# GpSimd adds all thirteen probability tiles of a group, and the row sums share a ring of five PSUM banks

## The chip, the cores and the metric

One core of a Trainium2 chip runs the whole kernel as one launch. The metric is device time in microseconds (us), the median of three runs. TensorE is called PE, VectorE DVE, ScalarE ACT, GpSimd POOL and the sync engine SP, as the profile has them.

## What is computed

The reference is a gated block on x (8 batches of 512 rows, width 512) with a context of 1601 rows per batch:

```python
q = qdq(layernorm(x)) @ qdq(wq).T + bq
k, v = split(ctx @ wkv.T + bkv)
attn = softmax(q k / sqrt(32))            # 16 heads of 32
x = x + tanh(g_xattn) * (qdq(attn @ v) @ qdq(wp).T + bp)
x = x + tanh(g_ffn) * (moe(layernorm(x)) + shared(layernorm(x)))
```

The softmax needs, for each head and each of 512 queries, the sum of the exponentials over 1601 context rows. How this sum is made is what the change touches.

## The kernel before, in words

The attention works by batch (8), by group of four heads (4), and by step: a step is one tile of 128 context rows, so a group has KT = 13 steps and the last tile has 65 rows. "Group 4.1" is group 1 of batch 4; there are 32 groups. The order of all engines is written out by hand and every engine walks it in its own program, tied to the others by semaphores.

In a step PE makes four score tiles (line 786, `scores_of`, two PSUM banks `s_ps`), ACT takes the exponential of each (line 965, `exp_of`) into one of three slots of `probs`, and PE multiplies them with the values (line 800, `heads_of`, one step late) into `o_ps`. Beside that each step carries tiles of other work (`lead_tiles`, `fill_tiles`) for the group that comes next: its k pieces and q (lines 698, 687), 64 tiles of scores whose row maxima DVE takes (lines 708 and 1184, steps 3 to 11), the context's transposes, the values, the output projection. All these tiles share a ring of NBANKS = 4 PSUM banks `r_ps`: tile n of the order uses bank n mod 4, and PE waits in `open_tile` until the tile four before it has been read.

The row sums are made in two ways. For ten of the thirteen steps POOL adds the four `probs` tiles to `prob_acc` (`add_probs`: a copy at step 0, line 1436, else an add, line 1439). For steps 4, 8 and 12 PE multiplies the tiles with ones into the bank `sum_ps` (line 812, `sums_of`, four matmuls that stand as x8 in the profile). After a group, PE adds `prob_acc` in the same way (line 820, `accumulated_sums`), at the end of step 0 of the next group, and ACT copies the bank to `sum_sb` (line 975, `copy_sums`). Only then may POOL begin the copy of the next group, since it overwrites `prob_acc`. ACT may reuse a slot of `probs` when PE has read the tiles of three steps before, and, for the ten steps, when POOL has added them.

In the step where POOL has nothing to add, step 4 of group 0, it adds a bias to the x rows (line 1446, `add_bias`). After the last group SP waits for the last sums (line 570) before it reads rows back into `prob_acc` and loads the shared weights; the feed-forward part and 32 experts follow, on the same ring.

The lines that set this:

```python
SBANKS, NBANKS, HALVES = 2, 4, 3
POOL_STEPS = [kt for kt in range(KT) if kt not in (4, 8, KT - 1)]
FIRST_SUMS = 4
```

Of the kernel before, what the change touches and what calls it, by code (L numbers as in the profile page):

```python
# [18 lines left out]
ALU = mybir.AluOpType  # L19
# [20 lines left out]
EPS = 1e-5  # L40
ROUND = 12582912.0
CT_SLOTS = 3
SBANKS, NBANKS, HALVES = 2, 4, 3
POOL_STEPS = [kt for kt in range(KT) if kt not in (4, 8, KT - 1)]
FIRST_SUMS = 4
MAX_STEPS = range(3, KT - 1)
V_AHEAD = 6
V_AT = {6: 1, 7: 2, 8: 4, 9: 5, 10: 7, 11: 8, 12: 10}
# [11 lines left out]
def rows(t):  # L60

    return min(P, M - t * P)


def group(b, g):

    return b * GROUPS + g


def step_of(b, g, kt):  # L70

    return group(b, g) * KT + kt
# [19 lines left out]
def head_tiles(b, g):  # L92
    return [("oT", b, g), ("sumT", b, g)]
# [73 lines left out]
class Ring:  # L167


    def __init__(self):  # L170
        order = [("setup", name, c) for name in ("wqT", "wpT", "wkT", "wvT") for c in range(DC)]
        order += [("setup", "gateT"), ("setup", "swp")]
        order += first_tiles()
        for at in steps():
            order += lead_tiles(*at) + fill_tiles(*at)
        order += head_tiles(B - 1, GROUPS - 1) + [("hT", 0, c) for c in range(DC)] + [("logits", 0)]
        for f in range(B):
            order += ffn_tiles(f)
        order += [("hgT", 0)]
        for e in range(E):  # L180
            order += [("eg", e), ("eu", e)] + ([("hgT", e + 1)] if e + 1 < E else []) + [("ey", e)]
        assert len(set(order)) == len(order)
        self.n = {key: i for i, key in enumerate(order)}
# [37 lines left out]
def build(nc, x, ctx_in, g_xattn, g_ffn, wq, bq, wkv, bkv, wp, bp, gate_w, gate_bias, w1, w2, w3,  # L221
# [16 lines left out]
    with ctx:  # L238
# [3 lines left out]
        def sem(name):  # L242
            return ctx.enter_context(nc.semaphore(name))
# [118 lines left out]
        s_ps = [ctx.enter_context(nc.psum_tensor(f"s_ps{j}", [P, 512], FP32)) for j in range(SBANKS)]  # L362
        r_ps = [ctx.enter_context(nc.psum_tensor(f"r_ps{i}", [P, 512], FP32)) for i in range(NBANKS)]
        o_ps = ctx.enter_context(nc.psum_tensor("o_ps", [P, 512], FP32))
        sum_ps = ctx.enter_context(nc.psum_tensor("sum_ps", [P, 512], FP32))


        consts_ready = sem("consts_ready")
# [33 lines left out]
        probs_ready = sem("probs_ready")  # L402
        probs_used = sem("probs_used")
        probs_added = sem("probs_added")
        acc_summed = sem("acc_summed")
        heads_copied = sem("heads_copied")
        sums_copied = sem("sums_copied")
        h_ready = sem("h_ready")
        h_out = sem("h_out")
        x1_out = sem("x1_out")  # L410
# [36 lines left out]
        def _(sp):  # L447
# [119 lines left out]

            sp.wait_ge(x_quantised, B)
            sp.dma_start(xin[:, :, :], x_v[B - 1]).then_inc(x_again, DMA)
            sp.wait_ge(acc_summed, B * GROUPS)  # L570
            ffn_in(0)
            for wt, src in ((sg, shared_gate), (su, shared_up), (sd, shared_down)):
                sp.dma_start(wt[:, :, :], src.rearrange("(c p) n -> p c n", p=P)).then_inc(shared_in, DMA)
# [31 lines left out]
        def _(pe):  # L605
# [43 lines left out]
            def tile(key):  # L649
# [67 lines left out]
                    for t in range(TT):  # L717
                        last = nc.tensor.transpose(ps[:, t * P:(t + 1) * P], oT_sb[:, t * P:(t + 1) * P], ident[:, :])
                elif kind == "sumT":
                    pe.wait_ge(sums_copied, group(b, key[2]) + 1)  # L720
                    ps = open_tile(*key)
                    for t in range(TT):
                        last = nc.tensor.matmul(ps[:, t * GH:(t + 1) * GH], sum_sb[:, t * P:(t + 1) * P],
# [65 lines left out]
            def heads_of(s):  # L789

                kt, b, g = s % KT, s // KT // GROUPS, s // KT % GROUPS
                w, slot = rows(kt), s % HALVES
                if kt == 0 and s:
                    pe.wait_ge(heads_copied, s // KT)
                if g == 0:
                    wait_read(pe, "v", b, kt)
                pe.wait_ge(probs_ready, s * GH + GH)
                for j in range(GH):
                    h = g * GH + j
                    last = nc.tensor.matmul(o_ps[j * DH:(j + 1) * DH, :], v_sb[0:w, kt, h * DH:(h + 1) * DH],  # L800
                                            probs[0:w, slot, j, :], start=(kt == 0), stop=(kt == KT - 1))
                if kt in POOL_STEPS:
                    last.then_inc(probs_used, 1)

            def sums_of(s):

                kt = s % KT
                w, slot = rows(kt), s % HALVES
                if kt == FIRST_SUMS and s >= KT:
                    pe.wait_ge(sums_copied, s // KT)  # L810
                for j in range(GH):
                    last = nc.tensor.matmul(sum_ps[j * DH:(j + 1) * DH, :], ones[0:w, :], probs[0:w, slot, j, :],  # L812
                                            start=(kt == FIRST_SUMS), stop=False)
                last.then_inc(probs_used, 1)

            def accumulated_sums(n):

                pe.wait_ge(probs_added, (n + 1) * len(POOL_STEPS) * GH)
                for j in range(GH):
                    last = nc.tensor.matmul(sum_ps[j * DH:(j + 1) * DH, :], ones[:, :], prob_acc[:, j, :],  # L820
                                            start=False, stop=True)
                last.then_inc(acc_summed, 1)

            for key in first_tiles():
                tile(key)
            for b, g, kt in steps():
                s = step_of(b, g, kt)
                fill = fill_tiles(b, g, kt)
                if kt == 0 and s:
                    heads_of(s - 1)  # L830
                    sums_of(s - 1)
                for key in lead_tiles(b, g, kt):
                    tile(key)
                for j in range(GH):
                    scores_of(s, g, j)
                    for key in fill[len(fill) * j // GH:len(fill) * (j + 1) // GH]:
                        tile(key)
                    if j == SBANKS - 1 and kt:
                        heads_of(s - 1)
                if kt and (kt - 1) not in POOL_STEPS:  # L840
                    sums_of(s - 1)
                if kt == 0 and s:
                    accumulated_sums(s // KT - 1)
            last_step = step_of(B - 1, GROUPS - 1, KT - 1)
            heads_of(last_step)
            sums_of(last_step)
# [39 lines left out]
        def _(act):  # L886
# [84 lines left out]

            def copy_sums(n):

                act.wait_ge(acc_summed, n + 1)
                nc.scalar.copy(sum_sb[:, :], sum_ps[:, :]).then_inc(sums_copied, 1)

            for key in first_tiles():
                tile(key)
# [2 lines left out]
            for b, g, kt in steps():  # L981
# [10 lines left out]
                if kt == 0 and s:  # L992
# [407 lines left out]
        def _(pool):  # L1400
# [24 lines left out]

            def add_probs(s):

                slot, n = s % HALVES, adds_before(s)
                first = s % KT == POOL_STEPS[0]
                if first and s >= KT:  # L1430
                    pool.wait_ge(acc_summed, s // KT)
                for j in range(GH):
                    pool.wait_ge(probs_ready, s * GH + j + 1)
                    if first:
                        step.carry_wait()
                        last = G.tensor_copy(prob_acc[:, j, :], probs[:, slot, j, :])  # L1436
                    else:
                        pool.wait_ge(probs_added, (n - 1) * GH + j + 1)
                        last = G.tensor_tensor(prob_acc[:, j, :], prob_acc[:, j, :], probs[:, slot, j, :], ALU.add)  # L1439
                    last.then_inc(probs_added, 1)  # L1440

            def add_bias(b):
# [6 lines left out]
                last.then_inc(x_biased, 1)  # L1449

            for b, g, kt in steps():
                if kt in POOL_STEPS:
                    add_probs(step_of(b, g, kt))
                elif g == 0 and kt == FIRST_SUMS and b:
                    add_bias(b - 1)
            add_bias(B - 1)

# [79 lines left out]
```

## Time and profile before

| what | value |
|---|---|
| median of 3 runs | 3401.5 us (3399.94 to 3410.48) |
| the profiled execution's own time | 3410.04 us |
| its span | 3408.1 us |
| TensorE clock granted, mean | 0.912 |
| before the first step | 0 to 139.3 us |
| attention steps | 139.3 to 2695.5 us |
| feed-forward | 2695.5 to 3156 us |
| experts | 3156 to 3408 us |

The last four lines are read from the trace at the first exponential, the end of the last sums, and the first expert's work. In the rows, "[2.26 <-DVE piece_max L1184]" says that the engine was idle for 2.26 us until that instruction ended. Several instructions of one kind that follow each other stand as one row with their count.

### The profile page before, as it was taken

To read this page: it belongs to the slowest core of one execution; us is meant where nothing else is said; L and a number is where in the kernel's file an instruction comes from. 1 tells how busy PE (TensorE), PEld (TensorE's weight loads), DVE (VectorE), ACT (ScalarE), POOL (GpSimd) and SP (SyncE) were. 2 spreads that over 40 slices of the span, in tenths; PEclk is the share of its full clock that TensorE was granted. 3 is DMA by queue.
4 is the path that set the end of the run, shared out by engine and by line. 5 is a ranking of instruction groups with operands and counts; after the bars stand their busy time and mean duration, and the time that the engine had idled before them with its cause. 6 is when DMAs were issued, how large, how long until landed. Compare 5 with 4: busy or idle time off the path is not lost. (4 is left out here: it accounts for less than half of the span.)

```text
span 3408.1 us, 43422 instructions
## 1 busy us (share of the span) xinstructions
PE 2915.5 (86%) x14836; PEld 1224.1 (36%) x14876; DVE 1958.9 (57%) x4052; ACT 1265.7 (37%) x2268; POOL 1826.3 (54%) x1570
## 2 busy tenths in 40 slices
PE   5997888888888887988798879888989879998787
PEld 3233333333333332333233333333333334443665
DVE  7667566756675667567666766675566143434122
ACT  2254435443544354445444534454345410100111
POOL 0285566456645575556465646564658613233555
PEclk9798999799979998998899979997999789999899
DMA  4111012110211031102110211121110221131897
GB/s 126 27 42 49 24 28 71 45 35 17 79 36 37 17 92 35 39 12 89 33 33 20 85 31 32 34 74 28 32 45 20 75 87 53 60 111 49 249 288 193
DMA packets 146651, 215.73 MB, mean 63 GB/s; under 512 B 25016, under 2 KB 78264, under 8 KB 146432
## 3 DMA queue, kind: packets, MB, share of 16 engines
q1 hardware_dynamic: 130560, 196.08, 19.1%
q0 software_dynamic: 15872, 16.87, 2.6%
q8 instruction: 120, 1.97, 0.2%
q14 instruction: 99, 0.81, 0.1%
HBM read 126.62 MB, written 34.37 MB: 47 GB/s over the span
## 5 line engine op out<-in xcount | busy, mean ns | idle before, releaser
L1439 POOL TENSOR_TENSOR prob_acc<-prob_acc,probs 128x512 f32<-128x512 f32 x1152 | 1449.4, 1289 | 614.4 <-ACT probs L965 614.1
L965 ACT ACTIVATE probs<-s_ps 128x512 f32<-128x512 f32 (+1 forms) x1664 | 942.9, 596 | 1091.6 <-PE s_ps L786 1060.9
L1184 DVE TENSOR_REDUCE piece_max<-r_ps 128x1 f32<-128x400 f32 (+1 forms) x2048 | 1025.2, 565 | 176.0 <-PE r_ps L708 172.6
L708 PE MATMUL r_ps<-k_flat,q_stack 96*128 96x400 f16 (+1 forms) x2048 | 637.4, 366 | 238.8 <-DVE piece_max L1184 138.2
L786 PE MATMUL s_ps<-q_stack,k_flat 97*128 97x512 f16 (+1 forms) x1664 | 649.8, 407 | 64.7 <-ACT probs L965 57.0
L800 PE MATMUL o_ps<-probs,v_sb 128*32 128x512 f32 (+1 forms) x3328 | 480.2, 651 | 19.8 <-ACT probs L965 19.8
L708 PEld LDWEIGHTS r_ps<-k_flat,q_stack 96*128 96x128 f16 x2048 | 205.1, 101 | 556.0 <-DVE piece_max L1184 268.4
L786 PEld LDWEIGHTS s_ps<-q_stack,k_flat 97*128 97x128 f16 (+1 forms) x1664 | 163.8, 103 | 645.6 <-ACT probs L965 389.6
L1436 POOL COPY prob_acc<-probs 128x512 f32<-128x512 f32 x128 | 72.8, 612 | 520.2 <-PE sum_ps L820 383.7
L1471 POOL DMA_INDIRECT slot_rows<-payload,slot x128 | 125.3, 979 | 315.0 <-DVE slot L1369 192.8
L1178 DVE SCALAR_TENSOR_TENSOR k_lo<-r_ps,bk_col,k_hi 128x400 f16<-128x400 f32 (+1 forms) x128 | 81.8, 639 | 333.2 <-ACT k_hi L923 333.2
L755 PE MATMUL r_ps<-probs,k_flat 128*128 128x512 f32 x512 | 230.6, 611 | 5.1 <-DVE sum_sb L1320 2.1
L1157 DVE TENSOR_TENSOR v_sb<-r_ps,bv_row 128x512 f32<-128x512 f32 (+1 forms) x104 | 71.9, 691 | 196.9 <-PE r_ps L669 196.8
L1497 POOL DMA_INDIRECT out_rows<-probs,slot_init x64 | 99.7, 1559 | 94.4 <-DMA out_rows<-probs,slot_init 56.6
L923 ACT ACTIVATE k_hi<-r_ps,bk_col 128x400 f16<-128x400 f32 (+1 forms) x128 | 76.5, 598 | 195.7 <-PE r_ps L698 195.7
L755 PEld LDWEIGHTS r_ps<-probs,k_flat 128*128 128x128 f32 x512 | 99.2, 196 | 130.2 <-issue 125.4
L669 PE MATMUL r_ps<-wkv_hi,ctx_hi 128*128 128x512 f16 (+1 forms) x416 | 124.9, 428 | 4.6 <-DVE ctx_lo L1150 2.4
L669 PE MATMUL r_ps<-wkv_hi,ctx_lo 128*128 128x512 f16 (+1 forms) x416 | 119.6, 414 | 0.0
L800 PEld LDWEIGHTS o_ps<-probs,v_sb 128*32 128x32 f32 (+1 forms) x3328 | 67.8, 111 | 138.6 <-issue 73.0
L812 PE MATMUL sum_ps<-probs,ones 128*32 128x512 f32 (+1 forms) x768 | 115.9, 678 | 0.0
L773 PE MATMUL r_ps<-k_flat,probs 128*128 128x512 f32 x256 | 112.8, 599 | 0.9 <-DVE probs L1325 0.9
L669 PE MATMUL r_ps<-wkv_lo,ctx_hi 128*128 128x512 f16 (+1 forms) x416 | 111.1, 391 | 0.0
(190 smaller groups left out, 2781.2 us busy)
## 6 DMA issues: line engine op xcount, KB each, us to landing
k_flat<-k_hi SPq DMA_DIRECT2D x256, 100.1 KB, 2.2
ctx_raw<-in_ctx SPq DMA_DIRECT2D x96, 256.0 KB, 2.7
v_sb<-in_L_ffn_w SPq DMA_DIRECT2D x48, 512.0 KB
xin<-in_x SPq DMA_DIRECT2D x16, 1024.0 KB, 5.5
k_flat<-k_lo SPq DMA_DIRECT2D x128, 100.1 KB, 2.2
ctx_hi<-in_L_ffn_w SPq DMA_DIRECT2D x24, 512.0 KB
ctx_lo<-in_L_ffn_w SPq DMA_DIRECT2D x24, 512.0 KB
q_stack<-q_hi SPq DMA_DIRECT2D x256, 32.0 KB, 1.9
```

The lines of the kernel that those rows point to most:

```text
L669: last = nc.tensor.matmul(ps[0:w, :], a[:, c, t * P:t * P + w], wt[:, 1, c, :], start=(n == 0), stop=(n == 3 * DC - 1))
L708: last = nc.tensor.matmul(ps[:, 0:w], q_stack[0:KSPLIT, g % 2, j, qt * P:(qt + 1) * P], k_stack[0:KSPLIT, g % 2, j, at:at + w], start=True ...
L755: last = nc.tensor.matmul(ps[:, :], wt[:, c, f * P:(f + 1) * P], hT[:, c, :], start=(c == 0), stop=(c == DC - 1))
L773: last = nc.tensor.matmul(ps[:, :], actT[:, f, t * P:(t + 1) * P], sd[:, f, :], start=(f == 0), stop=(f == FSC - 1))
L786: nc.tensor.matmul(s_ps[j % SBANKS][0:w, :], k_stack[:, g % 2, j, kt * P:kt * P + w], q_stack[:, g % 2, j, :], start=True, stop=True).then ...
L800: last = nc.tensor.matmul(o_ps[j * DH:(j + 1) * DH, :], v_sb[0:w, kt, h * DH:(h + 1) * DH], probs[0:w, slot, j, :], start=(kt == 0), stop= ...
L812: last = nc.tensor.matmul(sum_ps[j * DH:(j + 1) * DH, :], ones[0:w, :], probs[0:w, slot, j, :], start=(kt == FIRST_SUMS), stop=False)
L965: nc.scalar.activation(probs[0:w, slot, j, :], s_ps[j % SBANKS][0:w, :], ACT.Exp).then_inc(probs_ready, 1)
L1184: V.reduce_max(piece_max[:, j * TT + qt, i:i + 1], ps[:, 0:PIECE[i]], X_AXIS).then_inc(free_of(*key), 1)
L1439: last = G.tensor_tensor(prob_acc[:, j, :], prob_acc[:, j, :], probs[:, slot, j, :], ALU.add)
L1471: G.indirect_dma_start(out=slot_scr, out_offset=bass.IndirectOffsetOnAxis(ap=slot[:, t, k:k + 1], axis=0), in_=payload[:, t, k, :], in_off ...
L1497: G.indirect_dma_start(out=out, out_offset=bass.IndirectOffsetOnAxis(ap=e_slots[:, e, 0:1].bitcast(I32), axis=0), in_=e_y[e % 2][:, h * HA ...
```

## The change

`POOL_STEPS` becomes all thirteen steps, `sums_of` and its matmuls go, and NBANKS becomes 5: the bank `sum_ps` is now the fifth of the ring. The sums of `prob_acc` are a tile of that ring, ("acc", n), opened and closed like any other, with `start=True`. It stands at the end of step 1 of the next group instead of step 0 (ACC_AT), and so does ACT's copy. POOL's bias add stays in step 4 of group 0, behind that step's adds. POOL's copy and SP's read wait for the ring's semaphore of that tile in place of `acc_summed`.

```diff
-SBANKS, NBANKS, HALVES = 2, 4, 3
-POOL_STEPS = [kt for kt in range(KT) if kt not in (4, 8, KT - 1)]
-FIRST_SUMS = 4
+SBANKS, NBANKS, HALVES = 2, 5, 3
+POOL_STEPS = list(range(KT))
+BIAS_AT, ACC_AT = 4, 1
...
-    if kt in POOL_STEPS:
-        last.then_inc(probs_used, 1)
-def sums_of(s):
...
+    last.then_inc(probs_used, 1)
 def accumulated_sums(n):
     pe.wait_ge(probs_added, (n + 1) * len(POOL_STEPS) * GH)
+    ps = open_tile("acc", n)
     for j in range(GH):
-        last = nc.tensor.matmul(sum_ps[j * DH:(j + 1) * DH, :], ones[:, :], prob_acc[:, j, :],
-                                start=False, stop=True)
-    last.then_inc(acc_summed, 1)
+        last = nc.tensor.matmul(ps[j * DH:(j + 1) * DH, :], ones[:, :], prob_acc[:, j, :],
+                                start=True, stop=True)
+    close(last, "acc", n)
...
-                if kt and (kt - 1) not in POOL_STEPS:
-                    sums_of(s - 1)
-                if kt == 0 and s:
+                if kt == ACC_AT and s >= KT:
                     accumulated_sums(s // KT - 1)
...
 def add_probs(s):
-    slot, n = s % HALVES, adds_before(s)
+    slot, n, w = s % HALVES, adds_before(s), rows(s % KT)
     if first and s >= KT:
-        pool.wait_ge(acc_summed, s // KT)
+        key = ("acc", s // KT - 1)
+        pool.wait_ge(bank_full[ring.bank(*key)], ring.done(*key))
...
             for b, g, kt in steps():
-                if kt in POOL_STEPS:
-                    add_probs(step_of(b, g, kt))
-                elif g == 0 and kt == FIRST_SUMS and b:
+                add_probs(step_of(b, g, kt))
+                if g == 0 and kt == BIAS_AT and b:
                     add_bias(b - 1)
```

PE at the border between groups 0.1 and 0.2. L812 and L820 are the sums, L687 and L698 the next group's q and k pieces. Before:

```order
L800 MATMUL o_ps<-probs,v_sb 32x512 x4
L812 MATMUL sum_ps<-probs,ones 32x512 x4
L687 MATMUL r_ps<-qT_int,wqT 128x512 x4
...
L786 MATMUL s_ps<-q_stack,k_flat 128x512 x4
L820 MATMUL sum_ps<-prob_acc,ones 32x512 x4
L786 MATMUL s_ps<-q_stack,k_flat 128x512 x2
L698 MATMUL r_ps<-ctx_hi,wkv_hi 128x400 x4
```

Now:

```order
L800 MATMUL o_ps<-probs,v_sb 32x512 x4
L687 MATMUL r_ps<-qT_int,wqT 128x512 x4
...
L786 MATMUL s_ps<-q_stack,k_flat 128x512 x6
L698 MATMUL r_ps<-ctx_hi,wkv_hi 128x400 x4
...
L698 MATMUL r_ps<-ctx_hi,wkv_lo 128x400 x4
L809 MATMUL r_ps<-prob_acc,ones 32x512 x4
L786 MATMUL s_ps<-q_stack,k_flat 128x512
```

The last tile's sums are gone, and the sums of `prob_acc` have moved behind both k pieces of step 1, ahead of the first scores of step 2.

POOL over one group, before and then now:

```order
L1436 COPY prob_acc<-probs 128x512 x4
L1439 TENSOR_TENSOR prob_acc<-prob_acc,probs 128x512 x36
```

```order
L1422 COPY prob_acc<-probs 128x512 x4
L1425 TENSOR_TENSOR prob_acc<-prob_acc,probs 128x512 x44
L1425 TENSOR_TENSOR prob_acc<-prob_acc,probs 65x512 x4
```

Twelve adds are new per group, four of them on 65 partitions.

## Rows read from the trace of the kernel before

**Rows 1.** The page, busy time, share and instructions of each engine.
```profile
PE 2915.5 (86%) x14836; PEld 1224.1 (36%) x14876; DVE 1958.9 (57%) x4052; ACT 1265.7 (37%) x2268; POOL 1826.3 (54%) x1570
```

**Rows 2.** Stretches: all steps, groups 4.1, 4.3; us, busy PE, PEld, DVE, ACT, POOL.
```profile
139.30:2695.50 2556.20, 2216.77 (x11797) 814.20 (x11835) 1624.62 (x3042) 1162.28 (x2076) 1557.19 (x1310) 0.91 0.15 41
1519.00:1584.00 65.00, 57.07 (x316) 19.06 (x317) 45.15 (x91) 35.72 (x64) 46.81 (x40) 0.95 0.28 87
1677.70:1759.60 81.90, 70.97 (x391) 27.09 (x393) 46.76 (x88) 32.83 (x61) 47.54 (x40) 0.94 0.14 34
```

**Rows 3.** Groups of instructions: busy, mean ns, idle before and releaser.
```profile
L1439 POOL TENSOR_TENSOR prob_acc<-prob_acc,probs 128x512 f32<-128x512 f32 x1152 | 1449.4, 1289 | 614.4 <-ACT probs L965 614.1
L1184 DVE TENSOR_REDUCE piece_max<-r_ps 128x1 f32<-128x400 f32 (+1 forms) x2048 | 1025.2, 565 | 176.0 <-PE r_ps L708 172.6
```

**Rows 4.** GpSimd in order of time: start, us, count, idle before and releaser.
```profile
201.95 2.28 POOL L1436 COPY prob_acc<-probs 128x512 f32<-128x512 f32 x4 [9.54 <-PE sum_ps L820]
...
1521.78 2.28 POOL L1436 COPY prob_acc<-probs 128x512 f32<-128x512 f32 x4 [13.13 <-PE sum_ps L820]
1548.75 27.13 POOL L1439 TENSOR_TENSOR prob_acc<-prob_acc,probs 128x512 f32<-128x512 f32 x22 [0.87 <-ACT probs L965]
...
2590.10 2.27 POOL L1436 COPY prob_acc<-probs 128x512 f32<-128x512 f32 x4 [10.83 <-PE sum_ps L820]
...
2647.06 2.28 POOL L1436 COPY prob_acc<-probs 128x512 f32<-128x512 f32 x4 [6.50 <-PE sum_ps L820]
2649.30 44.18 POOL L1439 TENSOR_TENSOR prob_acc<-prob_acc,probs 128x512 f32<-128x512 f32 x36
```

**Rows 5.** TensorE in order of time, at two borders between groups.
```profile
1006.00 1.93 PE L812 MATMUL sum_ps<-probs,ones 65*32 65x512 f32 x8
...
2580.73 1.04 PE L812 MATMUL sum_ps<-probs,ones 65*32 65x512 f32 x8
...
2588.80 1.07 PE L820 MATMUL sum_ps<-prob_acc,ones 128*32 128x512 f32 x8
...
2595.17 0.84 PE L698 MATMUL r_ps<-ctx_hi,wkv_lo 128*128 128x400 f16 x4
```

**Rows 6.** ScalarE: last exponentials of group 1, batches 0 and 4.
```profile
250.81 1.07 ACT L965 ACTIVATE probs<-s_ps 65x512 f32<-65x512 f32 x2 [0.74 <-PE s_ps L786]
...
1575.34 1.07 ACT L965 ACTIVATE probs<-s_ps 65x512 f32<-65x512 f32 x2 [0.74 <-PE s_ps L786]
```

**Rows 7.** The chain of waits behind the last group: start, us.
```profile
2693.54 1.98 PE sum_ps L820 x8
...
2697.05 1.31 SPq L573
```

**Rows 8.** TensorE, group 0 of batch 7, at a wait and at two clocks.
```profile
2479.74 0.91 PE L708 MATMUL r_ps<-k_flat,q_stack 96*128 96x401 f16 x2 [2.26 <-DVE piece_max L1184]
...
2482.91 1.91 PE L669 MATMUL r_ps<-wkv_hi,ctx_lo 128*128 128x512 f16 x4
...
2492.16 1.03 PE L669 MATMUL r_ps<-wkv_lo,ctx_hi 128*128 128x512 f16 x4
```

**Rows 9.** VectorE in order of time: group 1, then group 2, of batch 4.
```profile
1552.46 12.42 DVE L1184 TENSOR_REDUCE piece_max<-r_ps 128x1 f32<-128x401 f32 x25 [0.52 <-PE r_ps L708]
1565.09 2.02 DVE L1184 TENSOR_REDUCE piece_max<-r_ps 128x1 f32<-128x400 f32 x4 [0.21 <-PE r_ps L708]
...
1622.92 3.69 DVE L1184 TENSOR_REDUCE piece_max<-r_ps 128x1 f32<-128x400 f32 x7 [0.30 <-PE r_ps L708]
...
1654.82 1.54 DVE L1184 TENSOR_REDUCE piece_max<-r_ps 128x1 f32<-128x400 f32 x3 [0.72 <-PE r_ps L708]
```

**Rows 10.** Who waited for whom: us in total, times, longest.
```profile
PE r_ps L708 <- DVE piece_max L1184: 138.2, 63, 3.0
...
PE r_ps L708 <- DMA q_stack<-q_lo: 54.6, 7, 8.7
```

**Rows 11.** One line of VectorE: duration min/median/max in ns.
```profile
L1041 DVE TENSOR_SCALAR xin<-xin x32: 426/428/1378, 62.3 to 2324.7; 128x512 f32<-128x512 f32 x32
```

More of the change, by code:

```diff
@@ L175, in __init__ @@
             order += lead_tiles(*at) + fill_tiles(*at)
-        order += head_tiles(B - 1, GROUPS - 1) + [("hT", 0, c) for c in range(DC)] + [("logits", 0)]
+            if at[2] == ACC_AT and step_of(*at) >= KT:
+                order += [("acc", step_of(*at) // KT - 1)]
+        order += [("acc", B * GROUPS - 1)] + head_tiles(B - 1, GROUPS - 1) + [("hT", 0, c) for c in range(DC)] + [("logits", 0)]
         for f in range(B):
@@ L364, in build @@
         o_ps = ctx.enter_context(nc.psum_tensor("o_ps", [P, 512], FP32))
-        sum_ps = ctx.enter_context(nc.psum_tensor("sum_ps", [P, 512], FP32))
         consts_ready = sem("consts_ready")
@@ L404, in build @@
         probs_added = sem("probs_added")
-        acc_summed = sem("acc_summed")
         heads_copied = sem("heads_copied")
-        sums_copied = sem("sums_copied")
         h_ready = sem("h_ready")
@@ L569, in _ @@
             sp.dma_start(xin[:, :, :], x_v[B - 1]).then_inc(x_again, DMA)
-            sp.wait_ge(acc_summed, B * GROUPS)
+            key = ("acc", B * GROUPS - 1)
+            sp.wait_ge(bank_full[ring.bank(*key)], ring.done(*key))
             ffn_in(0)
@@ L719, in tile @@
                 elif kind == "sumT":
-                    pe.wait_ge(sums_copied, group(b, key[2]) + 1)
+                    wait_read(pe, "acc", group(b, key[2]))
                     ps = open_tile(*key)
@@ L801, in heads_of @@
                                             probs[0:w, slot, j, :], start=(kt == 0), stop=(kt == KT - 1))
-                if kt in POOL_STEPS:
-                    last.then_inc(probs_used, 1)
-            def sums_of(s):
[L807 to L813, printed above, removed]
                 last.then_inc(probs_used, 1)
@@ L839, in _ @@
                         heads_of(s - 1)
-                if kt and (kt - 1) not in POOL_STEPS:
-                    sums_of(s - 1)
-                if kt == 0 and s:
+                if kt == ACC_AT and s >= KT:
                     accumulated_sums(s // KT - 1)
@@ L845, in _ @@
             heads_of(last_step)
-            sums_of(last_step)
             accumulated_sums(B * GROUPS - 1)
@@ L972, in copy_sums @@
             def copy_sums(n):
-                act.wait_ge(acc_summed, n + 1)
-                nc.scalar.copy(sum_sb[:, :], sum_ps[:, :]).then_inc(sums_copied, 1)
+                ps = full(act, "acc", n)
+                nc.scalar.copy(sum_sb[:, :], ps[:, :]).then_inc(free_of("acc", n), 1)
             for key in first_tiles():
@@ L991, in _ @@
                         tile(key)
-                if kt == 0 and s:
+                if kt == ACC_AT and s >= KT:
                     copy_sums(s // KT - 1)
@@ L1438, in add_probs @@
                         pool.wait_ge(probs_added, (n - 1) * GH + j + 1)
-                        last = G.tensor_tensor(prob_acc[:, j, :], prob_acc[:, j, :], probs[:, slot, j, :], ALU.add)
+                        last = G.tensor_tensor(prob_acc[0:w, j, :], prob_acc[0:w, j, :], probs[0:w, slot, j, :], ALU.add)
                     last.then_inc(probs_added, 1)
```

## Prediction

> **What bounds the kernel now.** I read the page first, then the stretches, the waits, and last the order of time at the places that the change touches. PE is busy for 86% of the span [rows 1]. In the attention steps, where the whole change lies, it is busy 2216.8 of 2556.2 us and POOL 1557.2, or 61% [rows 2]. But no engine bounds every step. PE waits for DVE's row maxima 138.2 us in 63 waits [rows 10], and DVE runs 25 maxima without a gap in 12.42 us, 0.50 us each [rows 9]. POOL does the same in the short steps: 22 adds in 27.13 us, and in the last group 36 adds in 44.18 us without a pause [rows 4]. That last group ends on POOL: PE's sums stand at 2693.54, right behind it, and the feed-forward's loads behind them [rows 7]. So PE, DVE and POOL are all near their limits, each in other steps, and I cost each place by the engine that is next. The profiled execution took 3410.04 us (span 3408.1); the median is 3401.5, so 8.5 less. I sum against 3410.04 and take the difference over to the median. A measurement here tells 0.3%, about 10 us, from no change.
>
> **What the change takes from PE.** A set of sums keeps PE for 1.0 us at the full clock and 1.9 at the half clock (rows of 1.04 and 1.93, whose ends overlap the next by a little) [rows 5].
> - The sums of the last tile stand between two groups, where PE runs without a gap, so they count in full. Of 31 borders I leave out the one before the last group, which POOL sets. Seven (behind group 2) run at the half clock: 23 x 1.0 + 7 x 1.87 = 36 us.
> - The accumulator's sums are only moved by a step. The k pieces of step 1 come 1.0 us earlier, the scores of step 2 do not. In group 3 PE waits for the DMA that stacks q and k, 54.6 us in 7 waits [rows 10], and that chain starts at the k pieces: there the moved sums hide in the wait, 7 x 1.0 = 7 us. SP's DMAs only follow.
> - The sums of tiles 4 and 8 are worth what DVE leaves. Group 1: 1.0 for the first, and 0.4 for the second, since DVE's gaps around it are 0.52 and 0.21 [rows 9]. Group 2: 0.30 and 0.72 are DVE's gaps behind them [rows 9]; I take 1.2 for both, as its sums run slowly. Group 0: a wait of 2.26 us for DVE stands behind the first [rows 8], so 0; the second 1.0. Group 3: DVE is busy 46.8 of 81.9 us [rows 2], so 1.0 and 0.8. That is 7 x (1.4 + 1.2 + 1.0 + 1.8) = 37.8, with group 0.0 (1.4) 39 us.
>
> Together 82 us. Bounds: 43 if DVE absorbs tiles 4 and 8, and 43 + 62 x 1.0 = 105 if nothing does.
>
> **What it gives to POOL.** 384 more adds. At 1449.4 / 1152 = 1.26 us [rows 3] that is 483 us and brings POOL to some 2040 us of the steps, 80%. Most lies beside longer steps. Where steps are short it does not. One group now costs POOL 4 copies (2.24 us from start to next start, 2647.06 to 2649.30) and 48 adds of 44.18 / 36 = 1.227, together 61.1 us [rows 4]. The adds on 65 partitions have no row: between half of 1.227 and all of it; I take all, as ACT's exponentials on 65 partitions take no less time (two in 1.07) [rows 6]. POOL also starts a group later, when the moved sums are done: behind the k pieces, 2595.17 + 0.84 less the overlap of 0.16 and the 1.07 that went ahead of them, then 1.07 and the 0.23 that the copy needed before (2588.80 + 1.07 to 2590.10), gives 2596.08 instead of 2590.10 [rows 4, 5]. That is 5.98 us later, in every group.
> - The last two groups. Copies at 2596.08, done at 2657.2; sums and 0.23, copies at 2658.5, done at 2719.6; the sums and their 1.98 us end at 2721.6. Before it was 2695.5 [rows 7]. So **+26 us**, all on the path.
> - Other groups: ACT's last exponential, step 12, may start when step 9 is added, 2.24 + 36 x 1.227 = 46.4 us after the copies begin. In group 0.1 that is 201.95 + 5.98 + 46.4 = 254.3 against 250.81 + 0.54 = 251.35 [rows 4, 6]: +3 us. In a group 1 it is 1521.78 + 5.98 + 46.4 = 1574.2 against 1575.88 - 1.4 = 1574.5: nothing, with the next term 0.5, so 3.5 us for seven. Groups 0, 2 and 3 are 81 us and more long; they hide it.
>
> POOL's in-order queue also puts the bias add behind four more adds; it has six steps until it is read, so nothing. ACT's copy stands before step 2 instead of inside step 1: in group 1 the table loads behind it start within 0.2 us of where they do now, as the moved sums' 1.07 us comes off ahead of it: nothing.
>
> **What DVE pays.** DVE's operations from SBUF to SBUF come in two lengths: one line has 428 ns as its median and 1378 as its longest [rows 11]. The long ones lie in stretches where POOL adds. 256 operations of four lines have this form; the mean of such a line is 840, so some 0.41 us each, 105 us in all, is lost now with POOL at 61%. At 80% that is 0.31 more, 32 us of DVE. In groups 0 and 2 DVE is what PE waits for, so I put 20 of the 32 on the path; bounds 0 and 138 (every one of them blocked, 256 x 0.95 - 105). The Trainium skill's page "SBUF — State Buffer", section "SBUF: two separate sides", has the rule behind it: DVE and GpSimd share one port pair as an exclusive lock, and the loser blocks for the whole instruction. It speaks against this change, and the trace agrees with its two lengths.
>
> The reported length of an add is a second such place: its mean is 1289 ns [rows 3] while the spacing is 1227 [rows 4]. I use the spacing. The skill's page "Perfetto Trace Analysis", section "GPSIMD Engine Instruction", says to do so. By the reported length a group would cost 3.0 us more: 6 in the last two and 36 x 0.062 = 2.2 in each of eight others, and the sum below would be 24 us higher.
>
> **What the fifth bank gives.** PE may be one tile further ahead when DVE is late. In each of 63 waits that is worth at most one max tile and its share of scores, about 0.4 us, 25 in all; at least 0. I take 10 for it.
>
> **Sum:** -82 + 26 + 3 + 3.5 + 20 - 10 = -39.5, so 3370.5 for an execution like the profiled one, and **3362 us** for the median.
>
> **The rivals.**
> 1. *The lock and DVE eat it (slower).* DVE absorbs the sums of tiles 4 and 8 (gain 43), the bank gives 0, and all 32 us of blocking land on the path: -43 + 32.5 + 32 = +21.5, 3423 us. For it: DVE's gapless maxima [rows 9]. Against: DVE still waits 176 us for PE's tiles [rows 3]. With the forecast's other terms it decides once the blocking on the path passes 59 us. Chance 0.11.
> 2. *No change.* Half of the gain of tiles 4 and 8 (20 us less), no bank, all 32: -62 + 32.5 + 32 = +2.5, 3404 us; with a little less of each about 3400. Chance 0.12.
> 3. *The fifth bank keeps PE fast.* Behind the 2.26 us wait PE's matmuls run at 1.91 us a row, later at 1.03: 1.2 and 2.4 GHz [rows 8]. If shorter waits let the clock stand in half of the 56 waits (of the 63) that lie in groups 0 and 2, each sparing some 1.3 us, that is 35 more: 3327 us. Against: a wait of 2.3 us only becomes 1.9. Chance 0.14.
> 4. *The forecast,* 0.63. Its own range is 3345 to 3385.
>
> **How the numbers follow.** Range 3327 to 3402: from rival 3 to rival 2. Faster by over 0.3%: 0.61 of the forecast and all of rival 3, 0.75. Within 0.3%: 0.12 and 0.02, 0.14. Slower: 0.11.
>
> **What would show it.** Right: the last sums end about 26 us later, counted from the start of group 7.2, with POOL gapless over both groups; groups 0, 2 and 3 shorter by 2 to 4 us and group 1 by about 2; POOL busy near 2040 us in the steps; the means of the 428 ns operations up from 840 toward 950; ACT waiting for POOL only in 0.1, 7.2 and 7.3. Wrong: groups of 81 us and more in which ACT waits for POOL, a mean of those DVE operations over 1.1 us, or groups 0 and 2 longer than before.

## The result, and the profile after

The changed kernel took 3516.4 us (median of 4 runs, 3513.0 to 3519.0) beside 3404.0 for the one before on the same chip: **1.0328 times as long, interval 1.0308 to 1.0348**. That is 112 us slower. The forecast was 3362, some 42 faster; the result lies outside its range and beyond the slower rival's 3423.

The page after, busy time of each engine, answers to [rows 1]:

```profile
PE 2868.9 (82%) x14108; PEld 1205.5 (34%) x14108; DVE 2174.2 (62%) x4052; ACT 1277.3 (36%) x2268; POOL 2317.9 (66%) x1954
```

The steps as one stretch (us, busy PE, PEld, DVE, ACT, POOL, clock), as in [rows 2]:

```profile
139.30:2800.00 2660.70, 2168.22 (x11057) 793.98 (x11057) 1840.32 (x3043) 1174.70 (x2077) 2041.96 (x1688) 0.89 0.15 40
```

POOL's 2042 us of the steps are what was forecast, and PE is busy for 49 us less. But DVE, which has the same 3042 instructions or one more, is busy 216 us longer. The last sums end at 2807.1 us instead of 2695.5: all of the loss lies in the steps, and what follows takes 5 us less (707.4 for 712.6).

Groups of instructions, busy and mean ns of one, idle before; the first answers to [rows 3]:

```profile
L1425 POOL TENSOR_TENSOR prob_acc<-prob_acc,probs 128x512 f32<-128x512 f32 (+1 forms) x1536 | 1935.4, 1292 | 279.5 <-ACT probs L950 278.1
...
L1154 DVE TENSOR_SCALAR qf<-qf,bq_col 128x512 f32<-128x512 f32 x32 | 124.3, 3884 | 1.1
...
L1015 DVE TENSOR_SCALAR so<-amax 128x4 f32<-128x4 f32 x8 | 41.5, 5191 | 0.3
L1026 DVE TENSOR_SCALAR xin<-xin 128x512 f32<-128x512 f32 x32 | 40.2, 1255 | 1.1
```

The add costs what it did. Line 1015, an operation on 4 columns, takes 5.2 us on average, and line 1154 3.9. Each line by itself, with the shortest, the median and the longest duration in ns:

```profile
L1154 DVE TENSOR_SCALAR qf<-qf,bq_col x32: 485/835/11360, 82.1 to 2666.2; 128x512 f32<-128x512 f32 x32
```
```profile
L1015 DVE TENSOR_SCALAR so<-amax x8: 169/7994/8008, 461.8 to 2812.6; 128x4 f32<-128x4 f32 x8
```

What one such hold looks like, in order of time (start, us, count, idle before), DVE, then POOL, then PE, in group 0 of batch 7:

```profile
2525.89 2.28 DVE L1013 TENSOR_REDUCE amax<-work 128x4 f32<-128x2048 f32 x1
2528.20 7.99 DVE L1015 TENSOR_SCALAR so<-amax 128x4 f32<-128x4 f32 x1
2536.22 0.18 DVE L1017 RECIPROCAL inv<-so 128x4 f32<-128x4 f32 x1
```
```profile
2525.14 11.02 POOL L1425 TENSOR_TENSOR prob_acc<-prob_acc,probs 128x512 f32<-128x512 f32 x9
```
```profile
2527.05 0.34 PE L708 MATMUL r_ps<-k_flat,q_stack 96*128 96x400 f16 x1
2537.07 0.52 PE L708 MATMUL r_ps<-k_flat,q_stack 96*128 96x401 f16 x1 [9.68 <-DVE piece_max L1169]
2537.38 0.63 PE L786 MATMUL s_ps<-q_stack,k_flat 97*128 97x512 f16 x1
```

DVE is not held for one add but until POOL's adds, which stand ready behind each other, are through (2536.16). PE has filled the ring and stands for 9.7 us. In the steps 18 operations take over 1.5 us longer than the shortest of their line, 165 us together; in the trace of before none does.

Who waited for whom, as in [rows 10]:

```profile
POOL prob_acc L1422 <- PE r_ps L809: 337.3, 31, 20.9
...
PE r_ps L708 <- DVE piece_max L1169: 209.7, 90, 10.6
...
ACT probs L950 <- POOL prob_acc L1425: 125.5, 139, 7.5
```

The last row is new in its size: before, ACT waited for POOL's adds 21.2 us in 21 waits. The first row is not: before, POOL waited 383.7 us in 31 borders for the sums. POOL idles less at the borders now, and what differs is when its idle time ends. Group 4.1 and the last two groups on POOL, which answer to [rows 4]:

```profile
1580.60 2.28 POOL L1422 COPY prob_acc<-probs 128x512 f32<-128x512 f32 x4 [14.40 <-PE r_ps L809]
1582.84 59.61 POOL L1425 TENSOR_TENSOR prob_acc<-prob_acc,probs 128x512 f32<-128x512 f32 x48
1644.57 2.27 POOL L1422 COPY prob_acc<-probs 128x512 f32<-128x512 f32 x4 [2.12 <-PE r_ps L809]
...
2680.80 2.27 POOL L1422 COPY prob_acc<-probs 128x512 f32<-128x512 f32 x4 [3.79 <-PE r_ps L809]
2683.03 58.85 POOL L1425 TENSOR_TENSOR prob_acc<-prob_acc,probs 128x512 f32<-128x512 f32 x48
2744.09 2.27 POOL L1422 COPY prob_acc<-probs 128x512 f32<-128x512 f32 x4 [2.21 <-PE r_ps L809]
```

In group 4.1 POOL waits 14.4 us and then runs 48 adds without one gap, since it never catches up with ACT. A run without a gap is not enough to hold DVE for long. The normalising operations of line 1080 on `work`, 28 of which begin in the first 11 us of such runs with two to five adds ready, were held for 0.84 to 0.96 us each:

```profile
L1080 DVE TENSOR_SCALAR work<-xin,mv,rstd x32: 542/1484/1500, 551.9 to 2868.5; 128x512 f32<-128x512 f32 x32
```

The holds of some 11 us on line 1154 come at the end of the run, with eight or nine adds ready, and each ends when these are through. From the starts of the exponentials and of POOL's copies (median of batches 1 to 6) I worked out when POOL ends a group and begins the next, counted from the next group's first exponential:

```
             behind group 0    behind 1       behind 2        behind 3
before       -10.4 / +2.7     -8.1 / +2.7    -16.5 / +2.7    -6.4 / +2.7
after         -3.3 / +11.1    +7.4 / +9.5     -6.7 / +10.4   +1.5 / +13.7
acc_at_0      -3.3 / +2.7     +6.6 / +8.9     -5.6 / +2.7    +1.5 / +2.8
```

In the pairs, the first number is when POOL ends its adds and the second when it begins the next copy. And the lengths of the groups in us (mean of batches 1 to 6), here also for runs that follow:

```
                      group 0    1      2      3
before                  93.7   65.0   93.6   81.0
after                  102.0   66.2   98.3   77.6
acc_at_0                95.4   60.8   99.5   77.8
ten_acc_at_0            88.8   60.5   93.5   77.9
short_groups_ten        94.5   61.5   91.4   77.4
serial_adds             96.5   73.7   89.3   77.8
q_in_psum              101.2   67.3   97.0   78.5
q_in_psum_serial_0      96.7   66.1   95.9   78.0
tail_only               93.3   65.1   91.3   80.6
tail_and_group_3        90.8   65.0   90.9   77.6
```

### The profile page after: what moved, and what is told of

Its sections match the earlier page's. It is cut to its first block and busy times, and to the rows that moved or that the text cites. A ratio compares the mean times of both kernels' runs of the same rounds, so it can differ in the third digit from the quotient of the medians.

```text
span 3514.5 us, 43010 instructions
## 1 busy us (share of the span) xinstructions
PE 2868.9 (82%) x14108; PEld 1205.5 (34%) x14108; DVE 2174.2 (62%) x4052; ACT 1277.3 (36%) x2268; POOL 2317.9 (66%) x1954
## 3 DMA queue, kind: packets, MB, share of 16 engines
q8 instruction: 114, 1.87, 0.2%
## 5 line engine op out<-in xcount | busy, mean ns | idle before, releaser
L1425 POOL TENSOR_TENSOR prob_acc<-prob_acc,probs 128x512 f32<-128x512 f32 (+1 forms) x1536 | 1935.4, 1292 | 279.5 <-ACT probs L950 278.1
L950 ACT ACTIVATE probs<-s_ps 128x512 f32<-128x512 f32 (+1 forms) x1664 | 952.8, 597 | 1138.5 <-PE s_ps L786 1003.0
L1169 DVE TENSOR_REDUCE piece_max<-r_ps 128x1 f32<-128x400 f32 (+1 forms) x2048 | 1014.4, 564 | 155.9 <-PE r_ps L708 154.0
L786 PE MATMUL s_ps<-q_stack,k_flat 97*128 97x512 f16 (+1 forms) x1664 | 668.7, 414 | 98.1 <-ACT probs L950 89.2
L800 PE MATMUL o_ps<-probs,v_sb 128*32 128x512 f32 (+1 forms) x3328 | 497.2, 673 | 30.4 <-ACT probs L950 30.4
L1154 DVE TENSOR_SCALAR qf<-qf,bq_col 128x512 f32<-128x512 f32 x32 | 124.3, 3884 | 1.1
L698 PE MATMUL r_ps<-ctx_hi,wkv_hi 128*128 128x400 f16 (+1 forms) x512 | 121.0, 363 | 3.2 <-DVE ctx_lo L1135 3.2
L698 PE MATMUL r_ps<-ctx_lo,wkv_hi 128*128 128x400 f16 (+1 forms) x512 | 123.0, 368 | 0.0
```

What stands on the lines that cost most here:

```text
L698: last = nc.tensor.matmul(ps[:, 0:w], wt[:, 0, c, g * P:(g + 1) * P], a[:, c, at:at + w], start=(n == 0), stop=(n == 3 * DC - 1))
L786: nc.tensor.matmul(s_ps[j % SBANKS][0:w, :], k_stack[:, g % 2, j, kt * P:kt * P + w], q_stack[:, g % 2, j, :], start=True, stop=True).then ...
L950: nc.scalar.activation(probs[0:w, slot, j, :], s_ps[j % SBANKS][0:w, :], ACT.Exp).then_inc(probs_ready, 1)
L1154: step.mark(V.tensor_scalar(qf[:, :], qf[:, :], SCALE, bq_col[:, g:g + 1], ALU.mult, ALU.add))
L1169: V.reduce_max(piece_max[:, j * TT + qt, i:i + 1], ps[:, 0:PIECE[i]], X_AXIS).then_inc(free_of(*key), 1)
L1425: last = G.tensor_tensor(prob_acc[0:w, j, :], prob_acc[0:w, j, :], probs[0:w, slot, j, :], ALU.add)
```

## The experiments

Ratios are to the kernel before, on the same chip, with their interval. A difference of 0.01 between two ratios is 34 us. Sums by group and by step are worked out from the profiled executions. "Hold" is used for a DVE operation that takes over 1.5 us longer than the shortest of its line.

### One part at a time

**ten_steps**

```diff
-POOL_STEPS = list(range(KT))
+POOL_STEPS = [kt for kt in range(KT) if kt not in (4, 8, KT - 1)]
```

> The changed kernel with GpSimd's adds cut back to the ten steps of before; the sums of tiles 4, 8 and 12 are left out altogether (a part of the softmax denominators is not computed). PE loses the 94 sets of sums, the fifth bank and the later accumulator stay. Theory (DVE is held by GpSimd's longer queues of adds): the load on GpSimd is that of before, so no hold of DVE is over 2 us, and the time is the 3404 of before less the 82 us of PE's sums, plus some 12 for the two last groups whose adds start 6 us later: 3325 to 3345. Rival B (the ring of five or the later accumulator is what costs): the time stays above 3400 though PE has less to do.

Measured: 3390.3 us, 0.9948 (0.9919 to 0.9977). Between theory and rival: without the extra adds the loss is gone, but some 50 us of PE's gain did not arrive either. Even with GpSimd's old load the theory's "no hold over 2 us" fails: there are eight holds, 65 us together, and in six of them line 1015 took 9.2 us. The rest of the change costs something too.

**serial_adds**

```diff
-pool.wait_ge(probs_added, (n - 1) * GH + j + 1)
+pool.wait_ge(probs_added, n * GH + j)
```

> The changed kernel, but each add waits until the add directly before it has ended (instead of the one four adds before), so GpSimd's adds are issued one by one. The same is computed. Theory (DVE is held through a run of adds that stand ready behind each other): a gap between adds lets DVE in, no hold is over 2 us, the mean of DVE's line for the bias of q falls from 3884 ns below 900, and the groups lose what they gained; against it the adds come slower, some 0.1 to 0.2 us each, which the last 96 adds pay in full: 3420 to 3450. Rival A (GpSimd's load bounds the groups): the adds come slower in all groups, and the time rises to 3540 or more. Rival C (the gaps don't matter, DVE is held by each add alone): no hold changes, about 3530.

Measured: 3508.2 us, 1.0309 (1.0273 to 1.0345): about as long as the change, between the theory and its rivals. What it does to DVE was as expected, the time was not. No hold is left:

```profile
L1154 DVE TENSOR_SCALAR qf<-qf,bq_col x32: 485/558/1591, 82.5 to 2639.7; 128x512 f32<-128x512 f32 x32
```

So the holds need adds that POOL may run straight behind each other, and groups 0 and 2 are shorter by 5.5 and 9.0 us. But 48 adds now take 67.5 us instead of 59.6, and group 1 is longer by 7.5:

```profile
2656.64 67.48 POOL L1425 TENSOR_TENSOR prob_acc<-prob_acc,probs 128x512 f32<-128x512 f32 x48
```

A short group follows POOL one for one. That was rival A's mechanism, in the short groups alone.

**four_banks**

```diff
-SBANKS, NBANKS, HALVES = 2, 5, 3
+SBANKS, NBANKS, HALVES = 2, 4, 3
```

> The changed kernel with four banks in the ring instead of five. The same is computed. Theory: the fifth bank lets PE run one tile further ahead while DVE is held, and it is worth 5 us in the feed-forward; without it 3522 to 3535, with the long holds of DVE unchanged. Rival B (the fifth bank harms, since DVE's work shifts against GpSimd's): 3500 or less.

Measured: 3553.8 us, 1.0424 (1.0389 to 1.0459). The fifth bank is worth 33 us in the changed kernel, more than the 6 to 19 expected. That it cushions DVE's holds is likely but not shown: the trace has 21 of them without the bank, 177 us together, for 18 and 165.

**acc_at_0**

```diff
-BIAS_AT, ACC_AT = 4, 1
+BIAS_AT, ACC_AT = 4, 0
```

> The changed kernel with the accumulator summed in step 0 of the next group, as before the change, instead of step 1. The same is computed. Theory: GpSimd's copies start some 6 us earlier in each group, so fewer adds stand ready behind each other at the places where DVE works on q, and the last two groups end 12 us earlier: 3470 to 3505. Rival B (the move itself is the cause): 3440 or less. If the start of the adds doesn't matter but for the last groups: 3504.

Measured: 3436.6 us, 1.0078 (1.0050 to 1.0106). Of the 112 us the moved accumulator alone carries 85. This is rival B's number. POOL begins at +2.7 us again, except behind group 1. The holds are not gone: 14 of 18 are left, 115 of 165 us. Those on q (line 1154, 9 to 11 us) stand as before, those in group 0 (lines 1015 and 1023) are down to 5. Between the two profiled executions, 69 us apart, the groups 0 are 50 us shorter in all and the groups 1 37 us; the groups 2 are 14 us longer, and the last two groups together differ by 1 us. In group 4.1, where the change had 48 adds in one piece, POOL is back to waiting for ACT once:

```profile
1541.97 2.28 POOL L1422 COPY prob_acc<-probs 128x512 f32<-128x512 f32 x4 [6.01 <-PE r_ps L809]
1544.20 4.96 POOL L1425 TENSOR_TENSOR prob_acc<-prob_acc,probs 128x512 f32<-128x512 f32 x4
1552.12 54.33 POOL L1425 TENSOR_TENSOR prob_acc<-prob_acc,probs 128x512 f32<-128x512 f32 x44 [2.95 <-ACT probs L950]
1608.66 2.28 POOL L1422 COPY prob_acc<-probs 128x512 f32<-128x512 f32 x4 [2.21 <-PE r_ps L809]
```

Behind group 1 PE stands for POOL instead, in step 0 of group 2:

```profile
1606.50 1.93 PE L809 MATMUL r_ps<-prob_acc,ones 128*32 128x512 f32 x8 [4.04 <-POOL prob_acc L1425]
```

That wait is 3.9 to 5.8 us behind the first group and behind every group 1, and 8.7 and 12.3 us behind the last two.

Part of the 85 is TensorE's clock. The first k piece of step 1 in group 4.1 with the stretch ahead of it, after the change and then with the sums in step 0 (us, busy PE, PEld, DVE, ACT, POOL, clock):

```profile
1569.50:1571.70 2.20, 1.17 (x3) 0.29 (x3) 2.10 (x4) 2.12 (x5) 0.00 (x0) 1.00 0.22 60
1571.80:1575.70 3.90, 3.90 (x13) 1.56 (x13) 1.20 (x6) 1.04 (x2) 0.00 (x0) 0.57 0.18 46
```
```profile
1539.20:1542.00 2.80, 2.04 (x12) 0.56 (x13) 2.64 (x5) 2.38 (x6) 0.03 (x1) 1.00 0.22 58
1542.10:1544.20 2.10, 2.10 (x13) 1.07 (x11) 0.66 (x5) 1.28 (x3) 2.10 (x4) 1.00 0.20 54
```

With the sums in between PE waits once for an exponential ahead of the piece (0.74 us; busy 2.04 of 2.80 us), and the piece runs at 2.4 GHz. With them moved, PE waits twice (0.74 and 0.26 us; busy 1.17 of 2.20 us), the granted clock is 0.57, mostly the 1.2 GHz level, and the same twelve matmuls take 3.78 us for 2.12. Over steps 0 and 1 of all groups TensorE stood at the 1.2 GHz level for 10 us before and 64 us after the change.

### The move and the load apart

**ten_acc_at_0** (ten_steps with `ACC_AT = 0`)

> As ten_steps (the sums of tiles 4, 8 and 12 are left out, so a part of the softmax denominators is not computed), but with the accumulator summed in step 0. GpSimd's load and the time at which it starts are those of before; PE has 94 sets of sums less and a fifth bank. If the late start of GpSimd's queue is what costs (ten_steps took 3390), this takes back 40 us or more: 3320 to 3350, with DVE's hold of 9 us on the scale line of group 0 gone. If PE's gain is simply absorbed by DVE, it stays at 3370 to 3390.

Measured: 3315.2 us, 0.9727 (0.9683 to 0.9771): theory, 5 us below its range. PE's sums and the fifth bank are worth 93 us, and the move costs 75 with ten adds, 85 with thirteen. No hold of over 1.5 us is left.

**stt_for_bias**

```diff
-V.tensor_scalar(qf[:, :], qf[:, :], SCALE, bq_col[:, g:g + 1], ALU.mult, ALU.add)
+V.scalar_tensor_tensor(out=qf[:, :], in0=qf[:, :], scalar=SCALE, in1=bq_col[:, g:g + 1].to_broadcast([P, 512]),
+                       op0=ALU.mult, op1=ALU.add)
```

> The changed kernel with one edit: the bias of q is added by DVE in another form (scalar_tensor_tensor with a broadcast column instead of tensor_scalar with two scalars), some 0.3 us longer by itself. The same is computed. Theory: the long holds fall on tensor_scalar (of 12 long holds on this line the longest was 11.4 us), the forms with two tensors were never held for more than one add; so they vanish here, or move in part to the cast behind it: 3440 to 3490. Rival: any operation of DVE from SBUF to SBUF is held until GpSimd's queue is empty: the holds stay on this line, 3516 to 3530.

Measured: 3522.8 us, 1.0335 (1.0283 to 1.0387), the rival. The other form is held just as long:

```profile
L1154 DVE SCALAR_TENSOR_TENSOR qf<-qf,bq_col x32: 691/1095/11611, 82.3 to 2667.0; 128x512 f32<-128x512 f32 x32
```

**acc_at_0_serial_02** (acc_at_0, and the wait of serial_adds where `s // KT % GROUPS in (0, 2)`)

> Two edits on the changed kernel: the accumulator is summed in step 0, and in groups 0 and 2 (the long ones) each add waits for the end of the one before it. The same is computed. Theory: the two losses are separate (the late start of GpSimd, 80 us by acc_at_0; the holds, which cost group 2 some 9 us and group 0 some 5 by serial_adds), and groups 1 and 3 keep their queued adds: 3436 less some 12 x 7 in group 2 and up to 3 x 7 in group 0 gives 3335 to 3380, below before. Rival (the slower adds of groups 0 and 2 carry over into the short groups): 3430 or more.

Measured: 3428.3 us, 1.0051 (1.0031 to 1.0071). A miss, and the rival's time, though not its mechanism: group 1 is 1.1 us longer (61.9), group 3 the same. Groups 0 and 2 lose only 2.6 and 3.2 us. The five holds in group 0 are gone; nine holds, 77 us, are left, all on q (line 1154), eight of them at the end of a group 1, where the adds are still queued. So this run does not say what those cost.

**tail_only** (the kernel before, with one part of the change)

```diff
-POOL_STEPS = [kt for kt in range(KT) if kt not in (4, 8, KT - 1)]
+POOL_STEPS = [kt for kt in range(KT) if kt not in (4, 8)]
...
-                    sums_of(s - 1)
```

> The kernel before with one part of the change alone: GpSimd adds the last tile of each group (eleven of thirteen), PE sums tiles 4 and 8 and the accumulator as before, four banks and the bank of the sums. The same is computed. By the prediction's own terms: 36 us less on PE, some 5 us more for each of the last two groups: 3375 to 3380. If GpSimd's longer queue holds DVE already here: 3400 or more.

Measured: 3378.2 us, 0.9917 (0.9879 to 0.9956), as expected. The term of the last tile stands by itself: in the traces the last step is 0.9 us shorter in groups 0, 1 and 3 and 2.2 in group 2, for the 1.0 and 1.87 of the forecast. Four holds are there, 11 us together.

### DVE's operands, the clock, a combination

**acc_0_q_in_psum**

```diff
-V.scalar_tensor_tensor(out=qf[:, :], in0=ps[:, :], scalar=swq[:, g:g + 1], in1=sx_row[:, :],
+V.scalar_tensor_tensor(out=ps[:, :], in0=ps[:, :], scalar=swq[:, g:g + 1], in1=sx_row[:, :],
...
+V.tensor_scalar(ps[:, :], ps[:, :], SCALE, bq_col[:, g:g + 1], ALU.mult, ALU.add)
+V.tensor_copy(q_hi[:, :], ps[:, :])
+V.tensor_tensor(q_lo[:, :], ps[:, :], q_hi[:, :], ALU.subtract).then_inc(free_of(*key), 1)
```

> Two edits on the changed kernel: the accumulator is summed in step 0, and DVE works q out in place in its PSUM bank, so that each of its four operations on q has a PSUM operand. The same is computed. In every trace so far no DVE operation with a PSUM operand was held, even with ten adds queued, and tensor_scalar and scalar_tensor_tensor from SBUF to SBUF both were. Theory: the hold of about 10 us on q in front of group 2 (step 0 of group 2 took 9.3 us instead of 3.1) goes: 3436 - 8 x 6 = 3375 to 3400. Rival (writing q_hi and q_lo to SBUF is enough to be held): about 3436 or more.

Measured: 3443.2 us, 1.0127 (1.0084 to 1.0169), the rival's time by another way (its runs scatter more than others, 3411 to 3452). The holds on q are all gone (the row of line 1154 is shown with q_in_psum below), yet step 0 of group 2 stays at 8.1 us: PE stands there for POOL's last add of group 1 anyway.

**scores_twice** (in step 0 of each group each score matmul is issued twice)

> The changed kernel, and in step 0 of each group PE computes each of the four scores twice over (the same result twice, some 0.9 us of PE more), to fill the place that the moved sums of the accumulator left. The same is computed. Clock theory: step 1 is 3 us longer since PE, with 1 us less to do in step 0, drops to the half clock in the k pieces behind it; with the filler step 1 falls from some 12.0 to 9.5 to 10.5 us in groups 0 and 1, and the time by 15 to 35 us. Rival (the filler is only more work for PE): step 1 stays at 11.5 or more, time 3516 to 3550.

Measured: 3502.7 us, 1.0300 (1.0253 to 1.0348). Step 1 fell from 11.7 to 10.1 us in group 0 and from 12.2 to 10.5 in group 1, as the clock theory has it; in group 4.1 the first k piece now shows a granted clock of 1.00 (0.57 above):

```profile
1569.00:1571.20 2.20, 2.20 (x13) 1.11 (x13) 0.95 (x5) 1.04 (x2) 0.00 (x0) 1.00 0.22 59
```

So more matmuls ahead of it cure the slow piece, and over steps 0 and 1 the time at the 1.2 GHz level falls from 64 to 14 us. The whole time is 10 to 14 us less, which is after the filler's own work is paid, and the two intervals overlap.

**acc_0_serial_q_last** (acc_at_0_serial_02 with q in PSUM; in the last group PE adds tiles 3, 5, 7, 9 and 11)

> Four edits on the changed kernel: the accumulator in step 0, queued adds only in groups 1 and 3, q worked out in PSUM, and in the very last group PE adds tiles 3, 5, 7, 9 and 11 itself, in the ring's bank of the accumulator. The same is computed. Theory: acc_at_0_serial_02 (3428) less 8 x 6 for q in front of group 2 and less 15 to 25 for the last group, where GpSimd has 20 adds of 1.23 us less behind the last exponential: 3355 to 3385, below the kernel before. If q's hold only moves on to the next operation from SBUF: 3400 or more.

Measured: 3410.0 us, 1.0005 (0.9984 to 1.0026). Only the last group's share came: between the two profiled executions the last two groups are 16 us shorter and the groups 2 only 2 us together. With the q holds gone PE still stands for POOL's last add in step 0 of group 2 (8.0 us), as in acc_0_q_in_psum.

### The shares, and a better kernel

**q_in_psum** (q in PSUM, the accumulator in step 1 as the change has it)

> The changed kernel with one edit: DVE works q out in its PSUM bank (accumulator in step 1, as the change has it). The same is computed. In acc_0_q_in_psum the holds on q were gone but the time was not, since PE waited for the same queued adds, for the accumulator at the end of step 0. Here that wait stands a step later, so the hold on q (11 us) is what makes the q stack late: step 3 of group 2 should fall from 16.7 to 11.7 us, eight times: 3465 to 3485. Rival (PE's wait for the accumulator at the end of step 1 takes over): 3500 to 3520.

Measured: 3535.0 us, 1.0356 (1.0333 to 1.0378): no gain, and beyond the rival too. Step 3 of group 2 fell from 16.7 to 10.3 us as expected (medians), but step 5 rose from 6.0 to 11.6: the hold had moved on to the next SBUF operation, the normalising of x. Line 1154, now with PSUM operands, and line 1080 (max 1496 ns after the change):

```profile
L1154 DVE TENSOR_SCALAR r_ps<-r_ps,bq_col x32: 758/759/760, 82.6 to 2675.0; 128x512 f32<-128x512 f32 x32
```
```profile
L1080 DVE TENSOR_SCALAR xin<-xin,mv,rstd x32: 534/1490/7364, 54.0 to 2379.3; 128x512 f32<-128x512 f32 x32
```

**q_in_psum_serial_0** (and the wait of serial_adds in group 0)

> As q_in_psum, and in group 0 of every batch each add waits for the one before it. The same is computed. Theory (the two long holds of the changed kernel are separate terms): group 0 falls from 102 to 96.5 us as in serial_adds, seven times, on top of q_in_psum: 38 us less than that run, 3425 to 3450. Rival: group 0 keeps its length, same as q_in_psum.

Measured: 3494.5 us, 1.0242 (1.0219 to 1.0265), 39 us less than q_in_psum: the expected 38, though from a higher start, so the time itself misses the range. The holds in group 0 (lines 1015 and 1023) are on the path at 4.5 to 5.5 us a group.

**short_groups_ten**

```diff
+def pooled(s):
+    n = s // KT
+    return s % KT not in (4, 8, KT - 1) or not (n % GROUPS == 1 or n in (0, B * GROUPS - 2, B * GROUPS - 1))
```

> The accumulator in step 0, all thirteen adds in groups 0, 2 and 3, but ten adds in the short groups (group 1 of each batch, the first group and the last two); the sums of tiles 4, 8 and 12 are left out there, so a part of the softmax denominators is not computed. Theory: a short group gives GpSimd 61 us of work in 60.5 us, so there the three more tiles are on the path one for one. acc_at_0 (3436) should come down by 6.5 us for each of eight groups 1 and by some 25 in the last two: 3350 to 3370; what is left to ten_acc_at_0 (3315) is single adds that hold DVE in groups 0 and 2. Rival (DVE's holds make up most): 3400 or more.

Measured: 3348.7 us, 0.9813 (0.9787 to 0.9839), at the theory's edge. The extra adds of the eleven short groups cost 90 us, those of the long ones 29 (to ten_acc_at_0). The 90 are not paid where the theory had them: to acc_at_0 the groups 1 themselves are only 6 us shorter in all, the groups 2 behind them 56, and the last two 32.

**tail_and_group_3** (tail_only, with tiles 4 and 8 on POOL in group 3 of batches 0 to 6)

> tail_only (3378), and in group 3, where GpSimd and DVE have room, tiles 4 and 8 are added by GpSimd too. The same is computed. Group 3 took 80.6 us in tail_only and 77.6 to 77.8 where GpSimd added all thirteen: seven groups, so 3355 to 3365. Rival (the 3 us came from the fifth bank): 3375 to 3380.

Measured: **3358.3 us, 0.9837 (0.9814 to 0.9860)**, 1.6% faster than the kernel before and faster than the change. The rival falls: group 3 went to 77.6 us on four banks. The 7 x 3.0 = 21 us of group 3 are the share that was expected; in the profiled executions group 0 is 2.5 us shorter as well, which is not explained.

## Why the prediction was wrong, step by step

The account in ratios of 3410 us, the load first and the move behind it:

```
PE's sums away and the fifth bank      -93   (ten_acc_at_0)
three more tiles, long groups          +29   (short_groups_ten over it)
three more tiles, short groups         +90   (acc_at_0 over short_groups_ten)
accumulator in step 1                  +85   (the change over acc_at_0)
sum                                   +111   (measured 112)
```

That the sum comes out is no check: each term is the difference between neighbours in one row of runs, and each holds in this order only (the move costs 75 us with ten adds).

- **What the change takes from PE: right in the sum, by luck in part.** Without the 7 for the move, 75 and 10 for the bank were forecast, and 93 measured. By group it is not as forecast: from before to ten_acc_at_0 group 0 gave 4.9 us for the forecast 2.0, group 1 4.5 for 2.4, and group 2 0.1 for 3.1; group 3 gave 3.1 for 2.8. How it splits between the sums and the bank is open: in the changed kernel the bank alone is worth 33. The last tile's 36 is the part that a run by itself bore out (tail_only).
- **"The accumulator's sums are only moved by a step": the step that failed most.** It was priced at -7, with POOL 5.98 us later, and it costs 85; groups of 81 us and more were said to hide that. POOL starts 7 to 11 us later, and the lateness is not hidden but turns into a backlog: ready adds, which hold DVE, and slots of `probs` that come free late (ACT's waits are 125.5 us, for 21.2 before). And the 1.07 us taken from step 0 were what kept PE's clock up: the first k piece of step 1 in group 4.1 did not come 1.0 us earlier; ACT's copy of it stands 6.4 us behind the group's first exponential, 5.1 before and in acc_at_0. How the 85 split is only estimated. For group 0's holds it is 39, measured on top of q_in_psum; in the traces step 4 of group 0 is 5.0 us longer than in acc_at_0, seven times. For the clock it is some 27, half of the 54 us more at the 1.2 GHz level in steps 0 and 1, if PE sets their pace. The last groups' late start, 2 x 5.98 in the forecast, adds nothing to acc_at_0: there the backlog of group 7.1 makes POOL begin just as late. What group 1 has of the 85 (5.4 us each) probably follows POOL's later start, but no run takes it apart.
- **What it gives to POOL: right at the end, too small elsewhere.** From the start of group 7.2 the last sums end 135.8 us later for 108.1 before, +27.7 where 26 was forecast. With the sums in step 0 it is +28.7, so the forecast's cause for 12 of the 26 is not a needed one. But for group 1 the term (3.5 us in all) looked at one consumer of the adds alone, the exponential that wants its slot, and found nothing. The other is PE, which wants the finished accumulator a few us into the next group. 61.1 us of POOL in a group of 61 to 65 us end 6.6 to 7.4 us inside the next. With the sums in step 0 that is PE's wait of 4 us in group 4.2, and group 2 is 8.1 us shorter when group 1 has ten adds. In all, the three tiles of the short groups cost 90 us, where 26 + 3 + 3.5 stood in the sum.
- **What DVE pays: wrong in its bound.** 20 us, with an upper bound for which every operation was blocked for 0.95 us, one add. That is what the trace of before showed: no operation there took over 1.2 us longer than the shortest of its line. With more adds ready one blocking took up to 10.9 us, so one add is no bound for it. The Trainium skill's page "SBUF — State Buffer", section "SBUF: two separate sides", has the loser block for the whole instruction; with serial adds the traces agree (line 1154 took 485 to 1591 ns, at most 1.1 us more, less than one add); with queued ones some operations waited for a whole run of adds (11360 ns).
- **The rival that was slower** had the right side and the right engine, but carried the same bound of one add and no late start, so it stopped at 3423. What was named as a sign of being wrong is what the trace shows: groups 0 and 2 longer, ACT waiting for POOL in long groups (3.4 us in group 4.0 for 0.9 before), a mean of 1255 ns on the 428 ns line.

## What to carry to other kernels

Before giving an in-order engine more work, find every consumer of its result and the earliest one; an engine at 80% over the whole can be over 100% in the short stages, and what it is late by there shows up in the next stage. A step that is moved to make room can be the one that starts another engine's queue: its price here was the backlog, not its own microsecond. And give such work away by stage: the adds of three tiles cost 90 us in the short groups, while those of two tiles gained 21 (7 x 3.0) in group 3.

## What the runs showed of the hardware

DVE operations from SBUF to SBUF took up to 12.0 us (line 1023 in q_in_psum, 0.48 at its shortest) while POOL ran through work that stood ready; with each add waiting for the one before, line 1154 took 1.6 us at most, where it took up to 11.4 after the change. Operations with a PSUM operand were never held: in none of the 17 traces did one in the steps take over 0.04 us longer than the shortest of its line and form (line 1154 took 758 to 760 ns in all 32 cases, where the longest of its SBUF form is that 11.4). Not every SBUF operation was held to the end of the queue: after the change casts of q (line 1156) were held 0.3 us with seven adds ready, seven times, and the normalising operations of line 1080 0.84 to 0.96 us with two to five. What decides that is open; the form of the operation (tensor_scalar or scalar_tensor_tensor on line 1154) does not.
